# A transformer kernel in which ScalarE takes some tensors from PSUM ahead of its exponentials

## The chip, the cores and the metric

The kernel runs on one core of one Trainium2 chip. The metric is the device time in microseconds (us). The kernel before takes 1423.8 us, the median of three runs (1423.69 to 1425.08).

## The reference

There are 16 sequences of 256 tokens with 256 channels each. A first part normalises them, conditions them on a subject and sends each token through two of eight experts (not touched here). A second part is one transformer layer with 16 heads of 16 channels:

```
x = ln(src) * (1 + scale) + shift
q, k, v = x @ Wq + bq, x @ Wk + bk, x @ Wv + bv           # 16 heads
scores = q k^T / 4 + attention_bias;  scores[mask] = -inf
ctx = softmax(scores) @ v
x = x + ctx @ Wo + bo
h = ln(x) * g2 + beta2
out = x + gelu2(h @ W1 + b1) @ W2 + b2                    # gelu2(u) = u * sigmoid(1.702 u)
```

The attention bias is a full array of 16 x 16 x 256 x 256 floats and is read once. Most matrix products are made in split precision: a tensor is cut into an upper part (rounded) and a lower part (what the rounding left), and products of the parts are added up in PSUM.

## The kernel before

Two parts run one behind the other; the change lies in the second, `transformer`. Its unit is a step `n`, which holds the 16 heads of sequence `n`, and spread over these 16 heads the work on its neighbours: the attention's end and the feed-forward of sequence `n - 1`, the queries, keys and values of `n + 1`, and the input of `n + 2`. Steps run from -2 to 17 (`entries`, L95): -2 to 2 and 13 to 17 are written out, 3 to 12 are a loop of two steps per turn. Each engine has its own list of instructions, run in the order in which they are written, and the engines meet only through semaphores: a wait holds up everything behind it on its engine.

For each head `h` of a step the engines do the following:

- PE: the scores of head `h + 2` into one of two banks `ps_s` (`scores`, L1349 and L1351; a bank is free once VectorE has read the head two before), then the turning of the probabilities of head `h` into `ps_p` (`turn_probs`, L1363; needs the exponentials of `h`, and the copy of head `h - 2` out of its bank), then what this head has of other work: queries at 0 (L1430), the reciprocals' spreading at 1 (L1400), keys at 2, the output product at 3 (L1420, L1421; needs `ctxT_ready`), values at 4 (L1438), turning of the normalised rows at 6 (`turn_h`, L1448), the four up products at 7 to 10 (L1463, L1467), the four down products at 11 to 14 (L1477), turning of the input at 15. At heads 1, 5, 9 and 13 it adds the weighting of four heads' values (`weigh`, L1379).
- VectorE: the minimum of head `h + 1` (`minimum`, L1586: bias minus scores, in place, with its row minimum), for heads 0 and 7 to 10 the copy of turned probabilities (L1592), then other work: the lower half of the queries at 1 (L1616; needs ScalarE's upper half), the scaling of the context at 2 (L1611; needs ScalarE's copy), the lower half of the keys at 3, the residual at 4 (L1633; needs the output product) with its moments (L1639 to L1645), the normalised rows at 5 (L1651; need POOL's root) and the values' copy (L1624), the lower half of the turned rows at 6 (L1656; needs ScalarE's upper half).
- ScalarE: the exponentials of head `h + 1` in two halves with their sums (`exponentials`, L1254; needs the minimum), for the other eleven heads the copy of turned probabilities (`take_probT`, L1260), and behind these the copies out of PSUM that the change moves: queries at 1 and keys at 3 (`upper`, L1278), the second half of the context at 2 (`take_ctx`, L1284), the turned rows at 6 (`take_hT`, L1289). At 8 to 11 come tanh (L1295, ahead of the exponentials) and the upper half of the activation (L1301), at 15 the modulated input (L1268).
- POOL: gathers of expert rows (L1191), roots (L1180), the sum `x3b` (L1210), the mask's conversion (L1205), lower halves of activations (L1198).
- SP: all loads and stores. Queries and keys go out to memory and come back in another layout, in 16 transfers.

Of the kernel before, what the change touches and what calls it, by code (L numbers as in the profile page):

```python
# [19 lines left out]
C = D // P  # L20
# [14 lines left out]
ADA_B, Q_B, K_B, FF_B1, LN2_G, LN2_B = 11, 15, 17, 19, 27, 29  # L35
# [48 lines left out]
def exists(n):  # L84

    return not isinstance(n, int) or 0 <= n < B
# [883 lines left out]
def by_scalar(h):  # L970
    return h not in BY_VECTOR
# [12 lines left out]
def transformer(nc, ctx, io, keep):  # L984
# [3 lines left out]
    def sem(name):  # L988
        if name not in sems:
            sems[name] = ctx.enter_context(nc.semaphore(name))  # L990
        return sems[name]

    def sb(name, shape, dt=F32):
        return ctx.enter_context(nc.sbuf_tensor(name, shape, dt))

    def bank(name):
        return ctx.enter_context(nc.psum_tensor(name, [P, 512], F32))

    const, vec, gates, out_row = keep["const"], keep["vec"], keep["gates"], keep["out_row"]
# [12 lines left out]
    q_b = sb("q_b", [P, C])  # L1012
# [42 lines left out]
    ps_out, ps_k, ps_q = [bank(n) for n in ("ps_out", "ps_k", "ps_q")]  # L1055
# [12 lines left out]
    def head_rows(h, j):  # L1068

        return bias[:, h // CHUNK % RING, h % CHUNK, j * T:(j + 1) * T]  # L1070
# [7 lines left out]
    def first_stack(eng, which):  # L1078

        eng.wait_ge(sem(f"{which}_split"), 2 * C)  # L1080
        for piece in ("hi", "lo"):
            name = f"{which}_{piece}"
            eng.dma_start(io[name].rearrange("(m p) t -> p m t", p=P), part[name][:].bitcast(F32)).then_inc(sem(f"{which}_sent"), 16)
        eng.wait_ge(sem("q_zeroed0"), 1)
        eng.wait_ge(sem(f"{which}_sent"), 32)
        for term in range(len(PASS_ROWS)):
            for i in range(2):
                dst, src = stack_rows(which, term, i, 0)
                eng.dma_start(dst, src).then_inc(sem("stack_in"), 16)
# [139 lines left out]
    def _(act):  # L1229
# [5 lines left out]
        def load_layer():  # L1235

            for c, dst in enumerate(raw):
                act.dma_start(dst, io["ff_w1"][:, c, :]).then_inc(sem("fold_in"), 16)
            for i, dst in enumerate(b1_row):
                act.dma_start(dst, io["ff_b1"][i * 512:(i + 1) * 512].partition_broadcast(P)).then_inc(sem("fold_in"), 16)  # L1240
            for i, dst in enumerate((bo, b2)):
                act.dma_start(dst[:], io["rows"][1 + i].partition_broadcast(P)).then_inc(sem("layer_in"), 16)
            act.dma_start(wo[:], io["wo"]).then_inc(sem("layer_in"), 16)
# [7 lines left out]
        def exponentials(n, h, par):  # L1251
            act.wait_ge(sem("neg_ready"), J * (H * n + h + 1))
            for j in range(J):
                act.activation(head_rows(h, j), head_rows(h, j), ACT.Exp, scale=-1.0,  # L1254
                               bias=neg_max[par][:, h, j:j + 1], accum_out=total[par][:, h, j:j + 1]).then_inc(sem("p_ready"), 1)
# [15 lines left out]
        def upper(n, which, bank, shift_by):  # L1271
            act.wait_ge(sem(f"{which}_done"), n + 1)
            if isinstance(n, int) and n == 1:
                act.wait_ge(sem(f"{which}_sent"), 32)
            elif at_least(n, 2):
                act.wait_ge(sem("split_sent"), 64 * (n - 1))
            for m in range(C):
                act.activation(part[f"{which}_hi"][:, m, :], bank[:, m * T:(m + 1) * T], ACT.Identity,  # L1278
                               bias=shift_by[:, m:m + 1]).then_inc(sem(f"{which}_split"), 1)

        def take_ctx(n, g):
            act.wait_ge(sem("pv_done"), GROUPS * n + (g + 1) * (GROUPS // 2))
            wait_free(act, sem("wo_done"), n)
            act.activation(ctxT[:, g, :], ps_ctx[:, g * T:(g + 1) * T], ACT.Copy).then_inc(sem("ctx_taken"), 1)  # L1284

        def take_hT(n):
            act.wait_ge(sem("h_turned"), n + 1)
            wait_free(act, sem("ff1_done"), 4 * n)
            act.activation(hT_part["hi"][:], halves(ps_k[:, :]), ACT.Identity, bias=1.0).then_inc(sem("hT_upper"), 1)  # L1289

        def tanh(n, pair):
            act.wait_ge(sem("ff1_done"), 4 * n + pair + 1)
            wait_free(act, sem("gelu_ready"), 4 * n + pair - 1)
            at = 2 * pair % 4
            act.activation(tanh_f[:, at:at + 2, :], halves(ps_up[pair % 2][:, :]), ACT.Tanh, scale=0.851).then_inc(sem("tanh2_ready"), 1)  # L1295

        def upper_gelu(n, pair):
            act.wait_ge(sem("gelu_ready"), 4 * n + pair + 1)
            wait_free(act, sem("ff2_done"), n)
            at = 2 * pair % 4  # L1300
            act.activation(act_part["hi"][:, 2 * pair:2 * pair + 2, :], up_f[:, at:at + 2, :], ACT.Copy).then_inc(sem("act_upper"), 1)  # L1301

        def step(n, par):
            starting = isinstance(n, int) and n == -1
            for h in range(H):
                ahead, head = neighbour(n, h, 1)
                if exists(n - 1) and 8 <= h < 12:
                    tanh(n - 1, h - 8)
                if exists(ahead):
                    exponentials(ahead, head, par if head else 1 - par)  # L1310
                if exists(n) and by_scalar(h):
                    take_probT(n, h)
                if h == 2 and exists(n - 1):
                    take_ctx(n - 1, 1)
                if isinstance(n, int) and n == 0 and h == 14:
                    load_w2()
                if isinstance(n, int) and n == 1 and h == 8:
                    act.wait_ge(sem("w2_lower"), 2)
                if h == 10 and exists(n):
                    take_ctx(n, 0)  # L1320
                if exists(n + 2) and h == (7 if starting else 15):
                    modulate(n + 2)
                if exists(n + 1):
                    if starting and h == 1:
                        act.wait_ge(sem("setup_done"), 1)
                    if h == 1:
                        upper(n + 1, "q", ps_q, q_b)
                    if h == 3:
                        upper(n + 1, "k", ps_k, vec[:, K_B:K_B + C])
                    if starting and h == 6:  # L1330
                        first_stack(act, "k")
                        load_layer()
                if exists(n - 1):
                    if h == 6:
                        take_hT(n - 1)
                    if 8 <= h < 12:
                        upper_gelu(n - 1, h - 8)

        entries(act, step)

# [551 lines left out]
```

## Time and profile before

| | |
|---|---|
| median of three runs | 1423.8 us |
| the profiled execution, its own time | 1427.18 us |
| its span, first to last instruction | 1425.4 us |
| PE busy, share of the span | 1276.8 us, 90% |
| VectorE (DVE) | 988.0 us, 69% |
| ScalarE (ACT) | 903.1 us, 63% |
| POOL | 665.1 us, 47% |
| mean granted clock of PE | 0.976 |

Times are from the span's start. PE's busy time is a sum of matmuls whose starts are recorded and whose ends are modelled, so two neighbours overlap in the rows; the distance between two starts is measured. In a timeline, a number in brackets is the idle time of the engine just ahead of the row, with the instruction that ended it. "issue" stands where nothing that the profile shows was waited for. VectorE is DVE and ScalarE is ACT in the rows; L1254 is line 1254 of the kernel.

### The profile page before, as it was taken

Reading aid. Unit: us, or ns where it says so; the run is one execution under the profiler, and the core shown is the slowest. Engines: PE = TensorE matmul, PEld = TensorE weight load, DVE = VectorE, ACT = ScalarE, POOL = GpSimd, SP = SyncE. Lnnn points to the kernel's source line nnn. Section 1 sums busy time; section 2 is a strip of 40 time slices with the busy share of each in tenths; the row PEclk is TensorE's granted clock in tenths of the full one; section 3 lists DMA queues with packets and bytes.
Section 4 is the critical chain, followed back from the end, with each engine's and each line's share of the span. In section 5 each row is a group of like instructions: output and inputs, shape, how many; then the busy total and the mean of one; then the engine's idle time right before and its main releaser. Section 6 shows DMA issues by size and latency. Waiting matters only on the chain. (4 is left out here: it accounts for less than half of the span.)

```text
span 1425.4 us, 34480 instructions
## 1 busy us (share of the span) xinstructions
PE 1276.8 (90%) x9923; PEld 1160.8 (81%) x9923; DVE 988.0 (69%) x2764; ACT 903.1 (63%) x2319; POOL 665.1 (47%) x580
## 2 busy tenths in 40 slices
PE   5884899999999999945899999999999999999996
PEld 4774899999999999944587888778877878788885
DVE  5776688889878987743776667566766667666652
ACT  3442677778777877722566676666666666667671
POOL 2775577787778777743032332332232232231221
PEclk9999999999999999976899999999999999999997
DMA  5885121121112111128766656655675556654620
GB/s 189 271 274 187 46 66 46 57 61 51 57 48 65 54 56 58 49 89 253 225 214 184 190 182 198 205 181 162 195 220 182 177 179 204 199 189 148 202 72 15
DMA packets 184707, 203.18 MB, mean 143 GB/s; under 512 B 18176, under 2 KB 172736, under 8 KB 184576
## 3 DMA queue, kind: packets, MB, share of 16 engines
q1 hardware_dynamic: 169136, 161.57, 36.9%
q10 hardware_dynamic: 9264, 23.47, 5.1%
q0 software_dynamic: 6176, 16.79, 3.4%
q14 instruction: 96, 0.79, 0.2%
q8 instruction: 35, 0.57, 0.2%
HBM read 155.89 MB, written 41.68 MB: 139 GB/s over the span
## 5 line engine op out<-in xcount | busy, mean ns | idle before, releaser
L1254 ACT ACTIVATE bias<-bias,neg_max 128x256 f32<-128x256 f32 x512 | 255.4, 501 | 193.7 <-DVE neg_max L1586 191.6
L343 POOL TENSOR_TENSOR w_lo<-w,w_hi 128x512 fp32r<-128x512 f32 x156 | 242.2, 1572 | 0.0
L1586 DVE CUSTOM_DVE_ANT_0 bias<-ps_s,bias 128x256 f32<-128x256 f32 x512 | 194.5, 417 | 34.0 <-PE ps_s L1351 21.4
L745 DVE TENSOR_TENSOR w_lo<-w,w_hi 128x512 fp32r<-128x512 f32 x156 | 149.8, 999 | 68.7 <-ACT w_hi L423 67.0
L544 PE MATMUL ps_y<-w_hi,hidT_hi 128*128 128x256 f32 x624 | 180.2, 289 | 1.9 <-DVE token_rows L759 1.9
L531 PE MATMUL ps_h<-htokT_hi,w_hi 128*128 128x256 f32 x624 | 178.5, 286 | 3.2 <-DVE htokT_lo L750 3.2
L531 PE MATMUL ps_h<-htokT_lo,w_hi 128*128 128x256 f32 x624 | 178.2, 286 | 0.0
L531 PE MATMUL ps_h<-htokT_hi,w_lo 128*128 128x256 f32 x624 | 178.1, 285 | 0.0
L1349 PE MATMUL ps_s<-mask_f,minus_ident 128*128 128x256 f32 x512 | 154.3, 323 | 25.6 <-DVE neg_max L1586 15.8
L544 PE MATMUL ps_y<-w_lo,hidT_hi 128*128 128x256 f32 x624 | 177.0, 284 | 0.0
L544 PE MATMUL ps_y<-w_hi,hidT_lo 128*128 128x256 f32 x624 | 177.0, 284 | 0.0
L1198 POOL TENSOR_TENSOR act_lo<-up_f,act_hi 128x512 fp32r<-128x512 f32 x64 | 82.6, 1291 | 198.1 <-ACT act_hi L1301 198.1
L1363 PE MATMUL ps_p<-const,bias 128*128 128x128 f32 x1024 | 158.7, 278 | 16.9 <-ACT bias L1254 15.6
L1349 PEld LDWEIGHTS ps_s<-mask_f,minus_ident 128*128 128x128 f32 x512 | 97.9, 191 | 59.1 <-DVE neg_max L1586 39.5
L1180 POOL TENSOR_TENSOR rstd<-mv,minus_half 128x2 f32<-128x2 f32 x32 | 23.2, 724 | 254.4 <-DVE mv L1645 179.9
L1363 PEld LDWEIGHTS ps_p<-const,bias 128*128 128x128 f32 x1024 | 116.6, 141 | 29.3 <-issue 17.9
L1351 PE MATMUL ps_s<-k_stack,q_stack 128*128 128x256 f32 x512 | 134.2, 284 | 0.0
L531 PEld LDWEIGHTS ps_h<-htokT_hi,w_hi 128*128 128x128 f32 x624 | 121.5, 195 | 3.9 <-DVE htokT_lo L750 3.9
L544 PEld LDWEIGHTS ps_y<-w_hi,hidT_hi 128*128 128x128 f32 x624 | 120.0, 192 | 2.1 <-DVE token_rows L759 2.1
L531 PEld LDWEIGHTS ps_h<-htokT_lo,w_hi 128*128 128x128 f32 x624 | 121.5, 195 | 0.0
L531 PEld LDWEIGHTS ps_h<-htokT_hi,w_lo 128*128 128x128 f32 x624 | 121.4, 195 | 0.0
L544 PEld LDWEIGHTS ps_y<-w_lo,hidT_hi 128*128 128x128 f32 x624 | 120.3, 193 | 0.0
(276 smaller groups left out, 3496.9 us busy)
## 6 DMA issues: line engine op xcount, KB each, us to landing
bias<-bias_dram SPq DMA_DIRECT2D x128, 512.0 KB, 4.2
w<-w_dram ACTq DMA_DIRECT2D x32, 512.0 KB
xin<-dispatch SPq DMA_DIRECT2D x39, 256.0 KB, 2.8
expert_out<-token_rows SPq DMA_DIRECT2D x39, 256.0 KB, 2.2
q_stack<-q_hi_rows SPq DMA_DIRECT2D x64, 128.0 KB, 2.9
q_stack<-q_lo_rows SPq DMA_DIRECT2D x64, 128.0 KB, 2.9
k_stack<-k_hi_rows SPq DMA_DIRECT2D x60, 128.0 KB, 2.8
k_stack<-k_lo_rows SPq DMA_DIRECT2D x60, 128.0 KB, 2.8
```

The source lines that it names most:

```text
L343: pool.tensor_tensor(w2_part["lo"][:, k, :], w2_piece(e, k), w2_part["hi"][:, k, :].bitcast(F32), ALU.subtract).then_inc(sem("w2_split"), 1)
L531: last = pe.matmul(ps_h[f // 2][:, (f % 2) * TOK:(f % 2 + 1) * TOK], w1_part[a][:, C * (f // 4) + c, (f % 4) * P:(f % 4 + 1) * P], htokT[b ...
L544: last = pe.matmul(ps_y[j][:, 0:D], hidT[a][:, f, j * P:(j + 1) * P], w2_part[b][:, k, (f % 2) * D:(f % 2 + 1) * D], start=(f == 0 and n = ...
L745: dve.tensor_tensor(w1_part["lo"][:, k, :], w1_piece(e, k), w1_part["hi"][:, k, :].bitcast(F32), ALU.subtract).then_inc(sem("w1_split"), 1)
L1180: pool.tensor_tensor(out[:], var[:, :, 1], minus_half[:], ALU.pow).then_inc(sem(done), 1)
L1198: pool.tensor_tensor(act_part["lo"][:, 2 * pair:2 * pair + 2, :], up_f[:, at:at + 2, :], act_part["hi"][:, 2 * pair:2 * pair + 2, :].bitca ...
L1254: act.activation(head_rows(h, j), head_rows(h, j), ACT.Exp, scale=-1.0, bias=neg_max[par][:, h, j:j + 1], accum_out=total[par][:, h, j:j + ...
L1349: pe.matmul(ps_s[h % 2][:, j * T:(j + 1) * T], minus_ident[:], mask_f[par][:, j, :], start=True, stop=False)
L1351: last = pe.matmul(ps_s[h % 2][:, j * T:(j + 1) * T], q_stack[par][:, h, j * P:(j + 1) * P].bitcast(F32R), k_stack[par][:, h // 2, :].bitc ...
L1363: last = pe.transpose(ps_p[h % 2][:, kt * T + j * P:kt * T + (j + 1) * P], head_rows(h, j)[:, kt * P:(kt + 1) * P], ident)
L1586: dve.tensor_tensor_reduce(head_rows(h, j), ps_s[h % 2][:, j * T:(j + 1) * T], head_rows(h, j), -1.0, LARGEST, ALU.add, ALU.min, neg_max[p ...
```

## The change

Inside ScalarE's list the order within a head changes; nothing is added or taken away, and no other engine's list is touched. `take_ctx` of head 2, the keys' `upper` of head 3 and `take_hT` of head 6 now stand ahead of the head's exponentials, and the queries' `upper` of head 1 stands behind the exponentials but ahead of the copy of probabilities.

```diff
                 if exists(n - 1) and 8 <= h < 12:
                     tanh(n - 1, h - 8)
+                if h == 2 and exists(n - 1):
+                    take_ctx(n - 1, 1)
+                if h == 3 and exists(n + 1):
+                    upper(n + 1, "k", ps_k, vec[:, K_B:K_B + C])
+                if h == 6 and exists(n - 1):
+                    take_hT(n - 1)
                 if exists(ahead):
                     exponentials(ahead, head, par if head else 1 - par)
+                if h == 1 and exists(n + 1):
+                    if starting:
+                        act.wait_ge(sem("setup_done"), 1)
+                    upper(n + 1, "q", ps_q, q_b)
                 if exists(n) and by_scalar(h):
                     take_probT(n, h)
-                if h == 2 and exists(n - 1):
-                    take_ctx(n - 1, 1)
...
-                if exists(n + 1):
-                    if starting and h == 1:
-                        act.wait_ge(sem("setup_done"), 1)
-                    if h == 1:
-                        upper(n + 1, "q", ps_q, q_b)
-                    if h == 3:
-                        upper(n + 1, "k", ps_k, vec[:, K_B:K_B + C])
-                    if starting and h == 6:
-                        first_stack(act, "k")
-                        load_layer()
-                if exists(n - 1):
-                    if h == 6:
-                        take_hT(n - 1)
-                    if 8 <= h < 12:
-                        upper_gelu(n - 1, h - 8)
+                if starting and h == 6:
+                    first_stack(act, "k")
+                    load_layer()
+                if exists(n - 1) and 8 <= h < 12:
+                    upper_gelu(n - 1, h - 8)
```

## Rows read from the trace of the kernel before

**Rows 1.** The page: busy shares, and 40 slices of the span.

```profile
PE 1276.8 (90%) x9923; PEld 1160.8 (81%) x9923; DVE 988.0 (69%) x2764; ACT 903.1 (63%) x2319; POOL 665.1 (47%) x580
...
PEclk9999999999999999976899999999999999999997
```

**Rows 2.** Windows of 14 steps: us, busy us per engine, clock, DMA.

```profile
sum 643.00, PE 603.76 PEld 518.12 DVE 429.50 ACT 426.68 POOL 188.96; mean PE 43.13 PEld 37.01 DVE 30.68 ACT 30.48 POOL 13.50
```

**Rows 3.** Waits of PE, 700 to 1400 us: total, times, longest.

```profile
PE ps_p L1363 <- ACT bias L1254: 13.5, 41, 0.4
PE ps_s L1349 <- DVE neg_max L1586: 12.8, 16, 1.6
PE ps_out L1420 <- DVE ctxT L1611: 8.3, 14, 1.3
```

**Rows 4.** Timeline of PE, step 7: start, us, instruction, idle before.

```profile
992.51 1.89 PE L1430 MATMUL ps_k<-xmT,wk 128*128 128x256 f32 x8
...
994.72 0.60 PE L1363 MATMUL ps_p<-const,bias 128*128 128x128 f32 x4
995.85 0.71 PE L1420 MATMUL ps_out<-wo,ctxT 128*128 128x128 f32 x4 [0.53 <-DVE ctxT L1611]
...
998.41 0.39 PE L1421 MATMUL ps_out<-const,xmT_kept 128*128 128x128 f32 x2
...
999.11 0.60 PE L1363 MATMUL ps_p<-const,bias 128*128 128x128 f32 x4
...
1004.58 0.65 PE L1363 MATMUL ps_p<-const,bias 128*128 128x128 f32 x4 [0.41 <-ACT bias L1254]
1005.30 0.66 PE L1448 MATMUL ps_k<-const,h_rows 128*128 128x128 f32 x4
1006.74 0.36 PE L1349 MATMUL ps_s<-mask_f,minus_ident 128*128 128x256 f32 x1 [0.78 <-DVE neg_max L1586]
...
1007.85 0.65 PE L1363 MATMUL ps_p<-const,bias 128*128 128x128 f32 x4 [0.40 <-ACT bias L1254]
...
1011.35 0.65 PE L1363 MATMUL ps_p<-const,bias 128*128 128x128 f32 x4 [0.21 <-ACT bias L1254]
1011.76 0.36 PE L1463 MATMUL ps_k<-hT_hi,ff_hi 128*128 128x256 f32 x1
...
1013.25 0.28 PE L1349 MATMUL ps_s<-mask_f,minus_ident 128*128 128x256 f32 x1
...
1013.72 0.60 PE L1363 MATMUL ps_p<-const,bias 128*128 128x128 f32 x4
```

**Rows 5.** Timeline of VectorE, same step.

```profile
1000.33 0.68 DVE L1633 TENSOR_TENSOR x<-ps_out,bo 128x512 f32<-128x512 f32 x1
...
1003.26 1.99 DVE L1651 TENSOR_SCALAR h_rows<-x,mv,rstd 128x256 f32<-128x256 f32 x2
...
1006.17 0.41 DVE L1586 CUSTOM_DVE_ANT_0 bias<-ps_s,bias 128x256 f32<-128x256 f32 x1
```

**Rows 6.** Timeline of ScalarE, same step.

```profile
994.63 0.37 ACT L1284 ACTIVATE ctxT<-ps_ctx 128x256 f32<-128x256 f32 x1
996.52 0.51 ACT L1254 ACTIVATE bias<-bias,neg_max 128x256 f32<-128x256 f32 x1 [1.51 <-DVE neg_max L1586]
...
997.99 0.82 ACT L1278 ACTIVATE k_hi<-ps_k,vec 128x256 fp32r<-128x256 f32 x2
...
1008.10 0.58 ACT L1289 ACTIVATE hT_hi<-ps_k 128x512 fp32r<-128x512 f32 x1
```

**Rows 7.** Groups by line, 700 to 1400 us: busy, mean ns.

```profile
L1576 DVE TENSOR_SCALAR xn<-src,mv,rstd 128x256 f32<-128x256 f32 x28 | 10.3, 411 | 0.8 <-POOL rstd L1180 0.7
```

**Rows 8.** Timeline of PE in step 1.

```profile
719.55 0.60 PE L1363 MATMUL ps_p<-const,bias 128*128 128x128 f32 x4
...
735.46 0.66 PE L1363 MATMUL ps_p<-const,bias 128*128 128x128 f32 x4
```

**Rows 9.** Timeline of POOL, step 7.

```profile
1004.45 1.53 POOL L1205 TENSOR_SCALAR mask_f<-mask 128x512 fp32r<-128x512 uint8 x1
```

## The prediction

> **What bounds the kernel now.** I read the page first, then windows of one step's length, PE's waits, and the timelines of the four compute engines through one step. The page has PE as the busiest engine, 90% of the span, and PE's granted clock at 9 (90% or more, the 2.4 GHz level) in every slice of the transformer but for some at its start and the last [rows 1]. Fourteen steps (one sequence each) fill 643.0 us, 45.93 us each, in which PE is busy 43.13, VectorE 30.68, ScalarE 30.48 and POOL 13.50 [rows 2]. So PE bounds, and what a reordering on ScalarE can win is PE's gaps alone. Three waits make nearly all of them: for exponentials (13.5 us), for VectorE's minima (12.8) and for the scaled context (8.3) [rows 3]. The timeline of PE puts them all into one stretch, from the turning of head 3's probabilities (994.72) to that of head 8's (1011.35); behind it, from 1011.76 on, instructions of the feed-forward follow each other without a gap [rows 4]. The stretch takes 16.63 us.
>
> The rows of VectorE and ScalarE tell why. ScalarE stands before each exponential for VectorE's minimum, and takes PSUM only behind the exponential. VectorE stands before each lower half, or before scaling the context, for just that ScalarE copy, and has the next minimum queued behind it. Context and keys are copied at 994.63 and 997.99 [rows 6], though PE had finished the keys at 992.51 + 1.89 = 994.40 [rows 4]; the minimum behind them is late, and VectorE comes to the residual (1000.33, [rows 5]) 1.53 us after the output product ended at 998.41 + 0.39 = 998.80 [rows 4]. Moments, head 6's minimum, the normalised rows, the values and head 7's minimum follow it on VectorE, and PE stands for the last one (0.78 at 1006.74).
>
> **The change, part by part.** No instruction is added or removed; no DMA moves, and SP's and POOL's queues keep their order. Four groups of copies move past an exponential or a copy on ScalarE. Times below count from the turning of head 3's probabilities in step 7 (994.72 = 0).
>
> Queries (head 1) go ahead of a copy of 0.5 us which PE wants only two heads later. VectorE's lower half of them and head 3's minimum come at least 0.5 us earlier. PE doesn't wait there now: cost nothing, gain nothing by itself. Below, it could cost what the delayed copy of 0.5 us takes if PE waited for it; PE has two heads of work as cover.
>
> Context (head 2) goes ahead of head 3's exponential. It no longer waits for head 3's minimum, only for the weighted sum that PE has then done, so it is ready over 2 us sooner, and PE's output product starts when the turning ahead of it is out of the way. Between 994.72 and 995.85 lie 1.13 us. A transposition set followed by free work needs about 0.44 (an estimate from 1011.35 to 1011.76, 0.41 [rows 4]). The gain is 0.69, more than the 0.53 shown as idle. The output product then ends at 0.44 + 2.95 = 3.39.
>
> Keys (head 3) go ahead of head 4's exponential. This adds a wait: everything on ScalarE stands until PE has made the keys, which is at 994.40, -0.32 on this scale. The copies end near 0.54 and the exponential (1.10 us for its halves: an estimate from 996.52 to the keys' copy at 997.99, less 0.48 for the copy between them, plus 0.1 for the end [rows 6]) at about 1.6. PE turns head 4 at 999.11 - 994.72 - 0.69 = 3.70: 2.1 us of cover. Were it gone, each us of delay would be a us of PE. VectorE's lower half (0.9) and head 5's minimum (0.77) end at about 2.2, 1.2 ahead of the output product's end. So from here the residual starts where its input ends, at 3.43, not at 5.61.
>
> The chain on VectorE from residual to head 7's second minimum runs from 1000.33 to 1006.17 + 0.41 = 1006.58, 6.25 us [rows 5], and I leave its length alone. Head 7's minimum is then there at 9.68.
>
> Turned rows (head 6) go ahead of head 7's exponential. PE turns them at 1005.30 now, 9.45 behind the output product's start. In that stand the flagged 0.41 before head 6 is turned [rows 4], and about 0.6 more by start-to-start distances against the same pairs elsewhere. It ends 0.66 later: at 0.44 + 9.45 - 1.0 + 0.66 = 9.55, or 10.14 if only the flagged part goes. I take 9.55, since starts are measured and ends are modelled. Now what was hidden is late: ScalarE copies the rows at 9.59 (0.58 us busy [rows 6]; what is queued behind starts some 0.48 after it) and begins head 7's exponential at 10.07, not at 9.72. It ends at 11.17, PE turns head 7 at 11.30, starts the first up product 0.41 later without a further wait (now 0.88 from 1007.85), needs 1.49 for it and 0.47 to the next turning [rows 4]: 13.67. So PE keeps two stalls, some 0.6 us for head 7's minimum and 0.9 us for its exponential. The stretch shrinks from 16.63 to 13.67, by 2.96 us; with the later end of the turned rows by 2.37. From head 8 on all engines run as now relative to PE. That includes tanh, which now waits for PE's product a little, where exponential 9 still has 0.8 us of slack.
>
> A rule of the Trainium skill speaks against such a sum. By the idle column the stretch holds 0.53 + 0.41 + 0.78 + 0.40 + 0.21 and little else, and the fourteen steps hold 643.0 - 603.8 = 39.2 us, 2.8 per step. That would be all there is to win, and with two stalls kept at most 1.5 per step. "Perfetto Trace Analysis", section "Identifying the Most-Contended Engine", holds that the busy share of matmuls is no measure of what PE has left, because pipelined instructions look otherwise in the trace than they cost. By the rule 2.96 may stand although the idle rows don't hold it; without it the sum is 21 us for fourteen steps.
>
> The sum. Steps 2 to 12 look alike: 11 x 2.9 = 31.9. Step 1 takes 735.46 - 719.55 = 15.91 for the stretch [rows 8]; splitting w2 on VectorE keeps its residual 0.7 late, so it ends at 14.35, gain 1.6. Steps 13 and 14 have a shorter stretch now, and I put them at 2.3 each; steps 0 and 15, with parts of the work only, at 1.3 each (estimates between 0 and 2.9). Step 16 has no exponentials: nothing. Together 31.9 + 1.6 + 4.6 + 2.6 = 40.7. The profiled execution took 1427.2 (span 1425.4 and 1.8 around it), so 1386.5; it lies 3.4 above the median of 1423.8, so I predict 1383.
>
> **The rivals.** Idle rows are right: 1.5 per step, 21 us, and 1402. For it: PE's modelled busy time. Against it: flagged idle of 0.53 at a distance 0.69 too long.
>
> Everything goes: start-to-start distances of the same pairs where nothing stalls add up to about 12.1 for the stretch (an estimate), 4.5 per step, over 60 us: 1361. Against it: head 7's exponential needs both turned rows and minimum, both tied to the output product.
>
> Given back: PE gets ahead and stands later for something tied to another clock, such as the bias transfers behind SP's queue or VectorE's start of each second step. Then it is near 1424. Against it: DMA is busy 0.6 of the time, and loads hang on PE's own progress.
>
> The slower side: the turned rows' copy blocks ScalarE. With the copy ahead, head 7's exponential can't start before PE has turned the rows. The turning hangs on VectorE's normalised rows, which take 1.99 for two where the same operation for the input takes 0.41 each [rows 5, 7], beside work of POOL. The point from which it decides is the turning's end at 12.5 (then nothing is left of 2.96); today it is 11.24. Were VectorE to stand behind POOL's mask too, 1.53 [rows 9], the end would come near 11.0 and the gain fall to 1.5. Only two such delays bring it to 13.0 and cost 0.5 a step: 1431. For it: the dependence runs through three engines. Against it: POOL's work keeps its distance to VectorE's.
>
> "SBUF — State Buffer", section "Who interferes with whom", in the Trainium skill has an exclusive port pair between VectorE and GpSimd, whichever starts first blocking the other for the whole instruction. The 1.99 against 0.82 agrees. By this rule alone a mask ahead of the rows would give the 1.5 per step above, near 1402.
>
> **How the numbers follow.** Forecast 0.68; idle rows (with the late turning and the mask case) 0.16; everything goes 0.04; given back 0.06, of which 0.04 within 0.2%; slower side 0.06. A gain per step of 2.0 to 3.4 over fourteen steps and the edges gives 1376 to 1394. The low end goes to 1374, the high end to 1408, which takes in the idle-row case and leaves out about 0.15. A measurement of this kernel tells 0.2%, some 3 us, from no change: faster 0.90, same 0.04, slower 0.06.
>
> **What would show it.** In the changed profile a step lasts 43.0 us. No wait of PE for ctxT is left at the output product. VectorE's residual starts within 0.1 us of the product's end. PE's waits before the scores of head 9 (0.6) and before turning head 7 (0.9) stay, and the wait before turning head 6, that before the first up product and that before turning head 8 are gone. ScalarE's idle time before turned rows and keys is charged to PE. It would be wrong if the residual still trails the product, if the VectorE chain grows beyond 6.3, or if new waits stand on PE behind head 8.

## The result and the profile after

The changed kernel takes 1380.9 us, the median of four runs (1379.99 to 1381.67), where the kernel before took 1424.4 on the same chip (four runs, 1423.69 to 1425.38): 0.969 of it, with a 95% interval of 0.968 to 0.971. The prediction was 1383. The profiled execution took 1381.58 with a span of 1379.8, 45.6 us less than that of before.

The page first, against [rows 1]. PE did the same 9923 matmuls at nearly the same clock digits, in less busy time (1254.1 for 1276.8), though nothing of its work was taken away:

```profile
PE 1254.1 (91%) x9923; PEld 1156.6 (84%) x9923; DVE 987.8 (72%) x2764; ACT 904.7 (66%) x2319; POOL 665.7 (48%) x580
...
PEclk9999999999999999996789999999999999999998
```

The windows of the same fourteen steps, against [rows 2]: their sum, busy time by engine, and the mean of a step.

```profile
sum 598.90, PE 582.24 PEld 515.21 DVE 431.09 ACT 426.03 POOL 190.78; mean PE 41.59 PEld 36.80 DVE 30.79 ACT 30.43 POOL 13.63
```

By these windows a step shrank from 45.93 to 42.78 us. Their first and last edges don't lie on the same instructions in the two traces, so their sums (643.0 and 598.9) don't give the gain exactly. From the turning of head 3's probabilities in step 1 to the same turning in step 15, fourteen steps later, it was 719.55 to 1357.40, 637.85 us, and is 718.37 to 1313.60, 595.23 us: 42.6 less. In these fourteen steps PE's busy time shrank from 598.6 to 578.6, by 20.0, and its idle time from 39.2 to 16.7, by 22.6. The other engines did the same work in nearly the same busy time. The span's 45.6 lies nearly all in these steps.

PE's waits from 700 to 1340 us (total, times, longest), against [rows 3]:

```profile
PE ps_p L1361 <- ACT bias L1254: 10.7, 18, 0.9
PE ps_s L1347 <- DVE neg_max L1584: 5.8, 13, 0.9
```

The wait for the scaled context is gone, that for the minima is 5.8 of 12.8 us, that for exponentials 10.7 of 13.5.

The timeline of PE through step 7, against [rows 4]. Times below count again from the turning of head 3's probabilities, here 975.19:

```profile
975.19 0.60 PE L1361 MATMUL ps_p<-const,bias 128*128 128x128 f32 x4
975.62 0.61 PE L1418 MATMUL ps_out<-wo,ctxT 128*128 128x128 f32 x4
...
978.08 0.39 PE L1419 MATMUL ps_out<-const,xmT_kept 128*128 128x128 f32 x2
...
983.95 0.60 PE L1446 MATMUL ps_k<-const,h_rows 128*128 128x128 f32 x4
985.08 0.35 PE L1347 MATMUL ps_s<-mask_f,minus_ident 128*128 128x256 f32 x1 [0.53 <-DVE neg_max L1584]
...
986.29 0.65 PE L1361 MATMUL ps_p<-const,bias 128*128 128x128 f32 x4 [0.50 <-ACT bias L1254]
986.70 0.37 PE L1461 MATMUL ps_q<-hT_hi,ff_hi 128*128 128x256 f32 x1
```

And the end of the stretch, the turning of head 8:

```profile
988.68 0.60 PE L1361 MATMUL ps_p<-const,bias 128*128 128x128 f32 x4
```

The output product starts at 0.43 (1.13 before). Its last pair ends at 978.08 + 0.39 = 3.28. The normalised rows are turned at 8.76, head 7's probabilities at 11.10, behind a wait of 0.50, and head 8's at 13.49. The stretch took 16.63. Of the stalls between, those before turning head 6, before the first up product and before turning head 8 are no longer there, those before the scores of head 9 (0.53) and before turning head 7 (0.50) are. In the other step of each turn of the loop they are 0.38 and 0.66, and the stretch is the same, 13.50.

VectorE in that step, against [rows 5]: the residual and head 7's second minimum.

```profile
978.66 0.69 DVE L1631 TENSOR_TENSOR x<-ps_out,bo 128x512 f32<-128x512 f32 x1 [1.32 <-PE ps_out L1419]
...
984.52 0.41 DVE L1584 CUSTOM_DVE_ANT_0 bias<-ps_s,bias 128x256 f32<-128x256 f32 x1
```

The residual starts at 3.47 and now waits for the product, 0.19 behind its end, where it had trailed it by 1.53. In the other step of each turn it is 0.04 behind.

ScalarE, against [rows 6]: the context, the keys, the turned rows and then head 7's exponential.

```profile
972.10 0.38 ACT L1284 ACTIVATE ctxT<-ps_ctx 128x256 f32<-128x256 f32 x1
...
974.91 0.84 ACT L1278 ACTIVATE k_hi<-ps_k,vec 128x256 fp32r<-128x256 f32 x2 [0.19 <-PE ps_k L1428]
...
984.59 0.60 ACT L1289 ACTIVATE hT_hi<-ps_k 128x512 fp32r<-128x512 f32 x1 [1.31 <-PE ps_k L1446]
985.08 0.50 ACT L1254 ACTIVATE bias<-bias,neg_max 128x256 f32<-128x256 f32 x1
```

The context is copied 3.09 ahead of the stretch's start, where it had been 0.09. The copies of the keys and of the turned rows now wait for PE and no longer for an exponential. The context's copy has no wait at all in this step and waits 1.27 for PE in the other step of the turn. The queries' copy still follows an exponential, as it was written. Head 7's exponential starts right behind the turned rows' copy, at 9.89.

### The profile page after: what moved, and what is told of

Its sections match the earlier page's. It is cut to its first block, busy times and chain, and to the rows that moved or that the text cites. A ratio compares the mean times of both kernels' runs of the same rounds, so it can differ in the third digit from the quotient of the medians.

```text
span 1379.8 us, 34480 instructions
## 1 busy us (share of the span) xinstructions
PE 1254.1 (91%) x9923; PEld 1156.6 (84%) x9923; DVE 987.8 (72%) x2764; ACT 904.7 (66%) x2319; POOL 665.7 (48%) x580
## 4 chain that ended last, share of the span: by engine, by line
PE 44%; issue 3%; ACT 3%; DVE 2%; DMA 1%; ACTq 1%; POOL 0%; POOLq 0%; DVEq 0%
PE ps_p L1361 8%; PE ps_s L1347 4%; PE ps_ctx L1377 4%; PE ps_s L1349 4%; PE ps_out L1475 3%; PE ps_q L1475 3%; PE ps_q L1428 2%; PE ps_q L1461 2%; PE ps_k L1461 2%; PE ps_k L1428 2%; PE ps_out L1418 2%; PE ps_q L1436 2%; ACT bias L1254 2%; PE ps_out L1398 1%; PE ps_q L1465 1%
## 5 line engine op out<-in xcount | busy, mean ns | idle before, releaser
L1260 ACT ACTIVATE probT<-ps_p 128x512 f32<-128x512 f32 x176 | 103.0, 585 | 30.8 <-PE ps_p L1361 30.7
L231 POOL TENSOR_TENSOR hidT_lo<-columns,hidT_hi 128x512 fp32r<-128x512 f32 x39 | 58.9, 1511 | 128.9 <-ACT hidT_hi L419 128.9
```

The source lines that it names most:

```text
L1260: act.activation(probT[:, h % (2 * GROUP), :, :], halves(ps_p[h % 2][:, :]), ACT.Copy).then_inc(sem("pT_scalar"), 1)
```

## The experiments

All medians are of four runs of the kernel. Each ratio is against runs of the kernel before on the same chip (1424.6 in the first four experiments, 1426.5 in the second four, 1427.5 in the third), with its 95% interval.

**One move at a time.** The theory: what a move is worth is read from distances between starts, and the moves overlap. The rival: PE's flagged idle time is all there is. Each of the first three kernels is the kernel before with one block moved, the fourth is the changed kernel with one moved back.

Context alone:

```diff
+                if h == 2 and exists(n - 1):
+                    take_ctx(n - 1, 1)
                 if exists(ahead):
                     exponentials(ahead, head, par if head else 1 - par)
                 if exists(n) and by_scalar(h):
                     take_probT(n, h)
-                if h == 2 and exists(n - 1):
-                    take_ctx(n - 1, 1)
```

> Kernel before, with only the context's copy moved ahead of head 3's exponentials. My theory (the four copies are links of one loop between ScalarE and VectorE, and PE gains what the whole loop gains, measured from start to start between the turnings of heads 3 and 8): PE's wait for ctxT goes, and with the context earlier head 4's minimum and the keys' copy come earlier too, so the residual starts 0.5 to 0.6 us behind the output product's end instead of 1.5. The stretch shrinks from 16.63 to about 14.9 us, 1.7 per step, time near 1399 to 1401 us. Rival (each copy is worth the PE wait that is charged to it): 0.5 to 0.7 per step, time near 1414 to 1416.

Measured: 1400.3 us, 0.982 [0.981, 0.984], 24.3 us of the 43.5. PE's timeline of step 7, then the row of VectorE's residual:

```profile
986.08 0.60 PE L1363 MATMUL ps_p<-const,bias 128*128 128x128 f32 x4
...
1000.82 0.65 PE L1363 MATMUL ps_p<-const,bias 128*128 128x128 f32 x4 [0.21 <-ACT bias L1254]
```

```profile
989.79 0.68 DVE L1633 TENSOR_TENSOR x<-ps_out,bo 128x512 f32<-128x512 f32 x1
```

The stretch is 14.74. The residual starts at 3.71. The product ended at 988.98 + 0.39 - 986.08 = 3.29, so it trails by 0.42. This move alone takes 0.69 from the product's start and 1.11 from the residual's trail, 1.80 of the 1.89 by which the stretch shrank. The time is the one that was told (1399 to 1401), and the rival's 1414 to 1416 is out.

Keys alone (the same with `if h == 3 and exists(n + 1): upper(n + 1, "k", ...)` ahead of the exponentials):

> Kernel before, with only the keys' copy moved ahead of head 4's exponentials. My theory: the wait for ctxT stays (1.1 us from the turning of head 3 to the output product), but the residual on VectorE starts at the product's end instead of 1.5 us behind it; the stretch shrinks to about 15.1 us, 1.5 per step, time near 1402 to 1404. Rival (worth by the PE wait charged to it): no PE wait is charged to the keys' copy, so no change, near 1424; and if PE's keys came late for ScalarE it would be slower.

Measured: 1402.2 us, 0.984 [0.982, 0.986], 22.4 us, though PE had no wait for keys to lose. PE, and the residual:

```profile
983.31 0.60 PE L1363 MATMUL ps_p<-const,bias 128*128 128x128 f32 x4
984.43 0.71 PE L1420 MATMUL ps_out<-wo,ctxT 128*128 128x128 f32 x4 [0.53 <-DVE ctxT L1611]
...
998.62 0.65 PE L1363 MATMUL ps_p<-const,bias 128*128 128x128 f32 x4 [0.19 <-ACT bias L1254]
```

```profile
987.58 0.69 DVE L1633 TENSOR_TENSOR x<-ps_out,bo 128x512 f32<-128x512 f32 x1 [1.04 <-PE ps_out L1421]
```

The product still starts at 1.12, behind its wait for the context. But the residual starts 0.2 behind its end (984.43 + 2.95 = 987.38). The trail of 1.53 shrank by 1.33, and the stretch by 1.32, to 15.31. So the delay of the minimum behind the keys' lower half was what held the residual, as the prediction said, and no wait of PE was ever charged to it. In the other step of each turn the product's start moved up as well, from 1.11 to 0.55, and the stretch shrank by 2.0, to 14.57. That part the theory didn't have.

Turned rows alone (`if h == 6 and exists(n - 1): take_hT(n - 1)` ahead of the exponentials):

> Kernel before, with only the turned rows' copy moved ahead of head 7's exponentials. My theory: here PE has turned the rows 0.6 us before head 7's minimum comes, so the copy fits into idle time of ScalarE and holds up no exponential; PE's wait before the first up product goes, and those for the lower half and for head 8's exponential; the stretch shrinks to about 15.5 us, 1.1 per step, time near 1408 to 1410. Rival (worth by the wait charged to it): 0.2 per step, near 1421. Second rival (the copy holds up the exponential): 1426 or more.

Measured: 1405.7 us, 0.988 [0.985, 0.990], 19.0 us, 3 more than the theory had. ScalarE around the copy, and the ends of the stretch on PE:

```profile
995.17 0.60 ACT L1289 ACTIVATE hT_hi<-ps_k 128x512 fp32r<-128x512 f32 x1 [1.07 <-PE ps_k L1448]
995.81 0.51 ACT L1254 ACTIVATE bias<-bias,neg_max 128x256 f32<-128x256 f32 x1
```

```profile
983.89 0.60 PE L1363 MATMUL ps_p<-const,bias 128*128 128x128 f32 x4
...
999.41 0.60 PE L1363 MATMUL ps_p<-const,bias 128*128 128x128 f32 x4
```

The stretch is 15.52. The copy fits into ScalarE's idle time before head 7's minimum: the exponential starts at 995.81, and head 7 is turned (997.03) at 13.14 as before (13.13). The slower side has nothing for it here. The 3 us more came in the other step of each turn, where the product's start moved up too (0.55 for 1.11), as in the keys' kernel. Why, I haven't followed. The four runs lie further apart than the others do, from 1403.9 to 1410.6.

All but the turned rows:

```diff
-                if h == 6 and exists(n - 1):
-                    take_hT(n - 1)
                 if exists(ahead):
                     exponentials(ahead, head, par if head else 1 - par)
...
+                if h == 6 and exists(n - 1):
+                    take_hT(n - 1)
```

> Changed kernel, with the turned rows' copy put back to where it was, behind head 7's exponentials and head 6's probabilities. My theory: head 7's exponential starts some 0.2 us earlier and PE turns head 7 at 10.95 instead of 11.11 (from the turning of head 3), but the first up product then waits for the copy (near 11.8), and head 8's minimum and exponential stand behind the lower half; the stretch is about 14.4 instead of 13.5, time near 1392 to 1395. Rival (the copy ahead of the exponential costs what it holds it up, the 0.5 to 0.8 us by which PE waits for head 7's exponential in the changed kernel): this kernel is faster than the changed one, near 1375 to 1380.

Measured: 1394.4 us, 0.979 [0.977, 0.980], in the range told (1392 to 1395), while the rival had 1375 to 1380. PE, then ScalarE:

```profile
979.41 0.60 PE L1361 MATMUL ps_p<-const,bias 128*128 128x128 f32 x4
...
990.43 0.65 PE L1361 MATMUL ps_p<-const,bias 128*128 128x128 f32 x4 [0.40 <-ACT bias L1254]
991.32 0.39 PE L1461 MATMUL ps_q<-hT_hi,ff_hi 128*128 128x256 f32 x1 [0.23 <-ACT hT_hi L1289]
...
993.93 0.65 PE L1361 MATMUL ps_p<-const,bias 128*128 128x128 f32 x4 [0.20 <-ACT bias L1254]
```

```profile
989.21 0.51 ACT L1254 ACTIVATE bias<-bias,neg_max 128x256 f32<-128x256 f32 x1 [1.71 <-DVE neg_max L1584]
...
990.68 0.58 ACT L1289 ACTIVATE hT_hi<-ps_k 128x512 fp32r<-128x512 f32 x1
```

Head 7's exponential waits for its minimum until 9.80. Head 7 is turned at 11.02, 0.08 earlier than with the copy ahead, and head 8 at 14.52, 1.03 later. Context, keys and queries together bring 30.3 us where context and keys alone bring 24.3 and 22.4: both remove the residual's trail, which can go only once. The last row but one of PE, the up product's wait for the turned rows (0.23), is a fifth of what the copy behind the exponentials costs.

**What holds the stretch now.** The theory: head 7's exponential is held by the turned rows' copy ahead of it. The rivals: the queries' move counts too, POOL's disturbance of the normalised rows holds the chain, or head 7's minimum does.

Queries back behind the copy of probabilities:

> Changed kernel, with the queries' copy put back behind the copy of head 1's probabilities. My theory: VectorE still has the scaled context 1.5 us or more ahead of PE's output product, so nothing moves: 1381, within 2 us. Rival (the queries' place is what starts the loop): VectorE gets to the context 0.5 to 1 us late and PE waits at the output product again, 1388 to 1395.

Measured: 1387.8 us, 0.972 [0.970, 0.974]. The changed kernel run again in the set after this one (below) has 0.9707 [0.969, 0.972]: no difference that can be told. The stretches of the loop's steps are alike (13.55 and 13.56) and PE doesn't wait at the output product; step 1 alone is 0.4 longer. The time told (1381, within 2 us) was missed by 7 us: it was set against the first run of the changed kernel, and that kernel takes 4.7 us longer in the set after this one (the last section). This holds for the next three kernels too.

POOL kept clear of VectorE's normalised rows, by the mask's conversion ahead of the root and the sum `x3b` behind the rows:

```diff
+            if exists(n + 1):
+                take_mask(n + 1, 1 - par)
             if exists(n - 1):
                 rsqrt(rstd2, mv2, "var2_ready", "rstd2_ready", n - 1)
+                pool.wait_ge(sem("h_rows_ready"), J * n)
                 prepare_sum(n - 1)
-            if exists(n + 1):
-                take_mask(n + 1, 1 - par)
```

> Changed kernel, with POOL's conversion of the mask moved ahead of the root and its sum x3b waiting until VectorE has made the normalised rows, so that these two rows meet no work on POOL. Both theories: the two instructions take about 0.8 us instead of 1.99 if POOL is what slows them. My theory: PE's wait for head 7's minimum (0.4 to 0.5 us) goes, but head 7's exponential still stands behind the turned rows' copy, whose input PE makes at its own time (8.76 from the turning of head 3), so PE waits as much more there: the stretch stays at 13.5 us and the time at 1381, within 3 us. Rival (worth by the wait charged to the minimum): 0.4 to 0.5 per step, 1374 to 1375.

Measured: 1385.8 us, 0.971 [0.969, 0.972], the same as the changed kernel run again (1385.6), though 5 us above the 1381 told. VectorE and PE in step 7:

```profile
983.85 0.73 DVE L1650 TENSOR_SCALAR h_rows<-x,mv,rstd 128x256 f32<-128x256 f32 x2
```

```profile
988.55 0.65 PE L1362 MATMUL ps_p<-const,bias 128*128 128x128 f32 x4 [1.27 <-ACT bias L1255]
```

The normalised rows take 0.73 there, not 1.99. PE's wait before the scores of head 9 is gone, and that before turning head 7 grew to 1.27: a stall went and came back one place on, and the stretch stayed at 13.5 (13.54, and 13.55 in the changed kernel run again). The rows are turned at 8.84 (8.83 in the changed kernel run again, 983.95 - 975.19 = 8.76 in its first run), right behind head 6's turning and without a wait in all three. So faster rows have nothing to shorten. What is left is a round trip, from PE's turning of the rows over ScalarE's copy and exponential back to PE, and PE has too little work to fill it.

Head 7's minimum ahead of the normalised rows on VectorE, and the turned rows' copy behind head 7's exponential but still ahead of the copy of probabilities:

```diff
-                if h == 6 and exists(n - 1):
-                    take_hT(n - 1)
                 if exists(ahead):
                     exponentials(ahead, head, par if head else 1 - par)
+                if h == 6 and exists(n - 1):
+                    take_hT(n - 1)
...
-                if exists(ahead):
+                if exists(ahead) and not (h == 6 and exists(n - 1)):
                     minimum(ahead, head, par if head else 1 - par)
...
                     if h == 5:
+                        if exists(n):
+                            minimum(n, 7, par)
                         normalise2(n - 1)
```

> Changed kernel with two orders changed: on VectorE head 7's minimum stands ahead of the normalised rows, and on ScalarE the turned rows' copy stands between head 7's exponentials and the copy of head 6's probabilities. My theory: both stalls left on PE, for head 7's minimum and exponential, go; the up product then waits for the turned rows until about 10.15 (from the turning of head 3), and head 8's exponential, behind the lower half and its minimum, ends at 12.55, so PE turns head 8 at 12.7 instead of 13.5: 0.8 per step, time near 1368 to 1371. Rival (the normalised rows, now 0.77 us later in VectorE's order, delay the turning and with it everything): 1381 or more.

Measured: 1374.7 us, 0.963 [0.961, 0.965], 10.9 below the changed kernel run again. Head 7 is turned at 9.75, without a wait, head 8 at 12.74. The size was missed by 4 to 7 us, mostly because I had set it against 1381.

The same, with head 8's minimum ahead of the turned rows' lower half as well:

> As e7_early_minimum, and on VectorE head 8's minimum stands ahead of the lower half of the turned rows. My theory: head 8's exponential then ends near 11.6 and PE turns head 8 at about 12.1 to 12.2, with at most 0.2 us of waiting at the lower half: 1.3 per step less than the changed kernel, time near 1361 to 1364. Rival (PE has no further gaps, or VectorE's later lower half costs what the minimum gains): same as e7_early_minimum, 1368 to 1371.

Measured: 1368.9 us, 0.958 [0.956, 0.961]; head 8 is turned at 12.30 to 12.38. It is over its range by 5 us, for the same reason and because head 8 was told for 12.1 to 12.2.

**Which half of the edit counts.** The last set runs the changed kernel and the one with two minima early again and takes the two halves of the early-minimum edit apart. The changed kernel:

> The changed kernel as it is, run again beside the others. In the last four kernels (e5, e6, e7, e11) ScalarE stands 2.4 to 3.6 us ahead of the context's copy in the ten steps of the loop, longer than PE's work explains, and PE waits 0.3 to 0.6 for head 3's exponential; the changed kernel and e1 to e4 show none of it. Theory A (it comes with the place of the run, not with the code): the wait is in all four kernels of this set or in none; with it the changed kernel takes 1384 to 1387, without it 1380 to 1382. Theory B (it comes with the code, by where instructions lie in memory): none in this kernel, wait again in r2_two_minima.

Measured: 1385.6 us, 0.971 [0.969, 0.972]. The first run of the same code had 0.969 [0.968, 0.971]. The wait is there this time, with the same code, as in the other three kernels of the set, and the time is in the range of theory A. Theory B has it absent here and is out.

Two minima early, again:

> e11_two_minima run again beside the changed kernel. Theory A: same wait of ScalarE ahead of the context's copy as in r1_changed of this set, and 14 to 17 us faster than that one either way (1.2 per step in the stretch). Theory B: wait present here, absent in r1_changed, so 10 to 12 us faster.

Measured: 1369.4 us, 0.959 [0.958, 0.961], 16.2 us below the changed kernel beside it, as theory A had it: the fastest kernel of all that were run. Step 6 on PE (turnings of heads 3, 7 and 8, at 0, 9.74 and 12.37):

```profile
930.13 0.65 PE L1361 MATMUL ps_p<-const,bias 128*128 128x128 f32 x4 [0.58 <-ACT bias L1254]
...
939.87 0.60 PE L1361 MATMUL ps_p<-const,bias 128*128 128x128 f32 x4
...
942.50 0.60 PE L1361 MATMUL ps_p<-const,bias 128*128 128x128 f32 x4
```

The minimum early, the copy where the change puts it (the VectorE half alone):

> Changed kernel with head 7's minimum ahead of the normalised rows on VectorE, and nothing else: ScalarE still copies the turned rows ahead of head 7's exponentials. My theory: the minimum is ready at 7.2 (from the turning of head 3) and of no use, since the exponential waits behind the copy until 9.9; PE's wait for the minimum goes and its wait for the exponential grows by as much; head 8 is turned at 13.5 and the time is that of r1_changed, within 2 us. Rival (the minimum is what holds PE): 0.4 to 0.5 per step less, 6 us.

Measured: 1384.6 us, 0.971 [0.969, 0.972], no gain: 1 us below the changed kernel, where up to 2 were told and the rival had 6. VectorE of step 6, then PE:

```profile
940.39 0.42 DVE L1584 CUSTOM_DVE_ANT_0 bias<-ps_s,bias 128x256 f32<-128x256 f32 x1
...
940.73 1.03 DVE L1649 TENSOR_SCALAR h_rows<-x,mv,rstd 128x256 f32<-128x256 f32 x2
```

```profile
933.44 0.65 PE L1361 MATMUL ps_p<-const,bias 128*128 128x128 f32 x4 [0.56 <-ACT bias L1254]
...
944.61 0.65 PE L1361 MATMUL ps_p<-const,bias 128*128 128x128 f32 x4 [1.27 <-ACT bias L1254]
...
946.99 0.60 PE L1361 MATMUL ps_p<-const,bias 128*128 128x128 f32 x4
```

The minimum is there at 7.4, ahead of the normalised rows, and it doesn't help: head 7's exponential stands behind the copy, PE waits 1.27, and the stretch is 13.55.

POOL kept clear, and the copy behind head 7's exponential, with the minimum where it was (the ScalarE half on top of the cleared rows):

> As e6_pool_clear, and the turned rows' copy stands between head 7's exponentials and the copy of head 6's probabilities. My theory (the exponential of head 7 is held by the copy of turned rows, and in e6 the earlier minimum was no use because of it): the exponential now starts with the minimum near 8.8 (from the turning of head 3), PE turns head 7 at about 10.0 instead of 11.1, and head 8 at about 13.1 instead of 13.5: 0.4 per step, 5 to 6 us less than r1_changed. Rival (order on ScalarE makes no difference with POOL cleared): same as r1_changed.

Measured: 1375.4 us, 0.964 [0.962, 0.966], 10.2 below the changed kernel. I had told 5 to 6, with head 7 at 10.0 and head 8 at 13.1; both came 0.3 or so sooner. VectorE, ScalarE and PE of step 6:

```profile
935.85 0.74 DVE L1650 TENSOR_SCALAR h_rows<-x,mv,rstd 128x256 f32<-128x256 f32 x2
```

```profile
937.97 0.51 ACT L1255 ACTIVATE bias<-bias,neg_max 128x256 f32<-128x256 f32 x1 [0.45 <-DVE neg_max L1585]
...
939.01 0.60 ACT L1290 ACTIVATE hT_hi<-ps_k 128x512 fp32r<-128x512 f32 x1
```

```profile
929.54 0.65 PE L1362 MATMUL ps_p<-const,bias 128*128 128x128 f32 x4 [0.59 <-ACT bias L1255]
...
939.29 0.60 PE L1362 MATMUL ps_p<-const,bias 128*128 128x128 f32 x4
...
942.28 0.65 PE L1362 MATMUL ps_p<-const,bias 128*128 128x128 f32 x4 [0.21 <-ACT bias L1255]
```

With the rows done in 0.74 the minimum behind them comes soon enough. The exponential starts at 8.43 and the copy follows it at 9.47; head 7 is turned at 9.75, head 8 at 12.74. So the exponential ahead of the copy is what both successful kernels share, with a minimum that is there by then, by being early or by cleared rows; neither is worth anything while the copy stands ahead. The copy right behind the exponential without either wasn't run. The kernel with all but the turned rows bounds it: the exponential stands for its minimum until 9.80 there, and head 7 is turned at 11.02. The copy directly behind it would start about 0.5 sooner than there, since only a copy of probabilities lies between, and head 8 would be turned near 14.0, later than 13.49 (an estimate from these rows). Both are needed, by that estimate; no run shows it.

## Why the prediction was right

The path was as told: context out of the way, then the residual at the product's end, the turned rows' end, head 7's exponential behind their copy, the up product. Its points, predicted and measured:

| | predicted | measured |
|---|---|---|
| output product ends | 3.39 | 3.28 |
| residual starts | 3.43 | 3.47 |
| head 7's minimum is there | 9.68 | 9.74 (984.52 + 0.41 - 975.19) |
| turned rows end | 9.55 | 9.36 (983.95 + 0.60 - 975.19) |
| head 7's exponential starts | 10.07 | 9.89 |
| head 7 is turned | 11.30 | 11.10 |
| head 8 is turned | 13.67 | 13.49 |
| PE's wait before the scores of head 9 | 0.6 | 0.53 |
| PE's wait before turning head 7 | 0.9 | 0.50 |
| a step | 43.0 | 42.8 (598.9 / 14) |

Of its signs one came only in half the steps: the residual was to start within 0.1 us of the product's end, and it starts 0.19 behind it in one step of each turn and 0.04 in the other.

**Idle rows against starts.** The rival that PE's idle rows are all there is fell. Idle time gave 22.6 of the 42.6 us of the fourteen steps, the rest was in rows counted as busy. By distances between the turnings of heads 3 and 8 before and after, 41.9 of the 42.6 is there: 3.1 us in each step from 2 to 12. The keys' experiment shows it without any wait of PE to take away. The rule of the Trainium skill ("Perfetto Trace Analysis", section "Identifying the Most-Contended Engine") held: the busy share of matmuls was no measure of what PE had left. The reason that the page gives, that pipelined instructions look smaller in the trace, isn't what these rows show: the same matmuls had 20.0 us more of busy time in the kernel that stalled more.

**Mis-sized terms.** The sum had 40.7 us and the span gave 45.6. Steps 2 to 12 gave 3.1 each and not 2.9, 34.3 for 31.9 us in all. It began with the output product ending 0.11 sooner, and the turning of the rows 0.2 sooner; I had taken only 1.0 off the way between the product's start and the rows, where 9.45 - 8.33 = 1.12 went. The stalls that were to stay came out shorter too, 0.53 and 0.50 for 0.6 and 0.9. Step 1 gave 2.5 for 1.6 (15.91 to 13.43): the splitting of w2 on VectorE, which I had put in its way, cost nothing, for the residual starts at 3.31 there. Steps 13 and 14 gave 2.8 and 2.3 (4.6 told for both), steps 0 and 15 1.2 and 1.7 (2.6 told). These add up to 44.8; the last 0.8 lies between stretches. Against the medians the gain was 43.5, since the profiled execution of before stood 2.7 above its median of four and that of the changed kernel 0.7 above its own. That is how 1383 came within 2.1 of 1380.9 on a sum that was 4.9 short: the mechanism was right, and that the number fits so closely is in part luck.

**The other rivals.** Everything goes (1361): with the copy ahead it can't, as head 7's exponential hangs on the turned rows; with two minima early and the copy behind, 16.2 us more went, of the 19.9 from the changed kernel's 1380.9 to it, and the stretch came to 12.37, near the 12.1 that the rival had. Given back: behind head 8 the steps run as before, and no new wait of PE stands there. The slower side needed the turned rows at 12.5. They were at 9.36. The price of its two delays by the mask was also added up wrongly: 9.55 + 2 x 1.53 is 12.6 and not 13.0, which would have cost 0.1 a step and not 0.5. The mechanism, the copy holding ScalarE, is real and is what bounds the stretch now. It costs 0.08 at the turning of head 7 against 1.11 that it saves behind it.

**POOL and the normalised rows.** They still take 1.99 for two beside POOL's sum `x3b` and its mask, and 0.74 without. The prediction priced a delay by the mask at its whole 1.53 us, and the rows show that most of the delay is the sum's. Step 15 has no mask to convert, and there the rows, begun beside the sum, take 1.68 already (kernel before, POOL and then VectorE):

```profile
1364.56 1.27 POOL L1210 TENSOR_TENSOR x3b<-x,b 128x512 f32<-128x512 f32 x1
```

```profile
1364.63 1.68 DVE L1651 TENSOR_SCALAR h_rows<-x,mv,rstd 128x256 f32<-128x256 f32 x2
```

So the sum adds 0.94 and the mask some 0.3. Where the minimum goes ahead of them (step 6 of the kernel with that alone, above), the rows meet only the last 0.25 of the sum and otherwise the mask, and take 1.03. The exclusive port pair in the Trainium skill ("SBUF — State Buffer", section "Who interferes with whom"), by which the one that comes second is blocked for the whole instruction, agrees with the sum's part (0.94 of the 1.20 that they overlap); beside the mask of 1.5 us the rows lose far less than that. The 1.25 us lie in VectorE's chain and yet were worth nothing in the changed kernel: PE turns the rows without a wait either way, and only the minimum comes sooner. Cleared rows with the copy behind the exponential are worth 10.2 us together; what is theirs alone there wasn't measured.

**Queries.** Cost and gain nothing: told, and not told apart from nothing.

## What to carry to other kernels

Where in-order engines hand each other work, write an engine's copy out of PSUM ahead of the work that waits for a slower partner, if its own input is there early; and behind it, if the input comes late. Here the same move was worth 24 and 22 us at two heads, and at the third its better place was directly behind the exponential once the minimum came early. Measure such a path by the distance between the same two starts of the bounding engine, in a stretch that stalls and in one that doesn't: the idle column held half of it. And try the moves together, since three single ones here added up to 65.7 us (24.3 + 22.4 + 19.0) and all four together were worth 43.5.

## What the hardware showed that I had not expected

In the second and third set ScalarE's copy of the context starts late, mostly behind a wait that the profile charges to "remote". Step 6 of the changed kernel, ScalarE and then PE, run again in the third set:

```profile
931.31 0.38 ACT L1284 ACTIVATE ctxT<-ps_ctx 128x256 f32<-128x256 f32 x1 [3.59 <-remote]
```

```profile
927.86 1.07 PE L1377 MATMUL ps_ctx<-probT,v_pad 128*32 128x256 f32 x16
...
932.80 0.65 PE L1361 MATMUL ps_p<-const,bias 128*128 128x128 f32 x4 [0.56 <-ACT bias L1254]
```

And the same rows in its first profile, with the same code:

```profile
929.00 0.39 ACT L1284 ACTIVATE ctxT<-ps_ctx 128x256 f32<-128x256 f32 x1 [1.27 <-PE ps_ctx L1377]
```

```profile
932.08 0.60 PE L1361 MATMUL ps_p<-const,bias 128*128 128x128 f32 x4
```

PE starts weighing the values (L1377) at 927.86 in both. The copy follows at 929.00 in the first and at 931.31 in the second, 2.3 us later. Head 3 is turned at 932.80 behind a wait of 0.56, not at 932.08.

From 700 to 1340 us there are 11 such waits of 31.2 us in all in the changed kernel run again, and 11 of 32.6 in the two-minima kernel beside it: in the ten steps of the loop and in step 13, which is written out. Steps 1 and 2, written out too, have the copy late as well, 2.4 and 2.2 us behind the weighing's start, where it is 1.14 in the same steps of the first profile, but their waits are charged to PE. Steps 14 and 15 have their 1.14. So it isn't a matter of the loop. The steps without it are those that gather no more input for a sequence two ahead; no run tests whether that is more than a coincidence. None of the first four experiments has it, though two of them copy the context in the same place of ScalarE's list.

From the weighing to the turning of head 3 the ten steps of the loop take 4.5 us more in all than in the first profile (0 to 0.77 each), and their stretches 0.06 more each, which together is about the 4.7 us between the two medians of one code (1380.9 and 1385.6). The kernel before rose by 3.1 in the same sets (1424.4 to 1427.5). The first four experiments ran on another chip than the second and third set; on which chip the first run of the changed kernel was isn't known. So the chip may be what differs, but chip and time changed together. What lies behind the word "remote" no run here shows; I have no cause for it.
